# A small silu behind the first FFN's gelus, and a layernorm divided around the second join's copies

## The reference

```python
x = x + 0.5 * ffn(layernorm(x))            # first FFN  ("f1")
x = x + attn(layernorm(x))                 # gated delta rule, 8 heads, then a gelu MLP ("M")
x = x + 0.5 * ffn(layernorm(x))            # second FFN ("f2")

def ffn(x):                                # 128 -> 512 -> 512 -> 512 -> 128
    h = silu(tlin(x, w1)) * tlin(x, w2)
    h = gelu(tlin(h, h1)); h = gelu(tlin(h, h2))
    return tlin(h, w3)
```

## Time and profile before

| | us |
|---|---|
| median of 3 runs | 1373.7 (1373.3 to 1374.37) |
| the profiled execution, its own time | 1375.78 |
| its span, first to last instruction | 1374.0 |
| PE busy | 1343.2 |
| DVE busy | 836.8 |
| ACT busy | 664.2 |
| POOL busy | 569.3 |

### The profile page before, as it was taken

The page is one execution under the profiler, slowest core; times in us unless marked ns, Lnnn a source line. Parts: engine busy times, 40 slices in busy tenths (PEclk is TensorE's granted clock), DMA queues, the critical chain, the costliest instruction groups (busy, mean ns, idle before and its releaser), DMA issues.

```text
span 1374.0 us, 26425 instructions
## 1 busy us (share of the span) xinstructions
PE 1343.2 (98%) x10358; PEld 916.4 (67%) x10358; DVE 836.8 (61%) x2502; ACT 664.2 (48%) x1132; POOL 569.3 (41%) x646
## 2 busy tenths in 40 slices
PE   9999999999999999999999999999999999999998
PEld 5466686547855588556775568655686647865887
DVE  4477786456774577744776457755586446874441
ACT  2476656236642466425573256622566136652233
POOL 0038353822448144561346614385142832467100
PEclk9999999999999999999999999999999999999999
DMA  6030355332563234650447314463155532651000
GB/s 188 25 99 4 102 121 122 84 88 71 131 120 96 51 93 127 119 112 27 122 104 142 84 31 112 105 138 89 40 124 118 91 89 71 146 116 44 23 1 8
DMA packets 351980, 122.99 MB, mean 90 GB/s; under 512 B 317936, under 2 KB 333040, under 8 KB 351856
## 3 DMA queue, kind: packets, MB, share of 16 engines
q1 hardware_dynamic: 351856, 121.30, 37.5%
HBM read 78.53 MB, written 42.73 MB: 88 GB/s over the span
## 4 chain that ended last, share of the span: by engine, by line
PE 61%; issue 15%; POOL 13%; DVE 7%; DMA 3%; ACT 2%; SPq 0%; POOLq 0%; DVEq 0%; ACTq 0%
PE bank L1488 16%; PE bank L1615 8%; POOL blkT L632 5%; POOL blkP L629 5%; PE bank L1734 4%; PE bank L1725 4%; PE bank L1698 4%; PE bank L1640 3%; PE bank L1526 3%; PE bank L1715 3%; PE bank L1689 2%; PE bank L1706 2%; PE bank L1496 2%; POOL QET L613 2%; PE bank L1839 1%
## 5 line engine op out<-in xcount | busy, mean ns | idle before, releaser
L1488 PE MATMUL bank<-big,h 128*128 128x512 f32 (+1 forms) x1056 | 442.1, 569 | 2.7 <-DVE TB L1047 2.5
L1488 PEld LDWEIGHTS bank<-big,h 128*128 128x128 f32 x1056 | 196.0, 190 | 204.0 <-issue 194.1
L586 POOL TENSOR_TENSOR rnorm<-ssq,mhalf 128x16 f32<-128x16 f32 (+1 forms) x35 | 84.0, 2401 | 418.6 <-DVE ssq L893 418.6
L1615 PE MATMUL bank<-wqkv,nT 128*128 128x512 f32 x336 | 162.2, 603 | 1.1 <-ACT V L1309 1.1
L632 POOL TENSOR_TENSOR blkT<-blkT,blkP 128x31 f32<-128x31 f32 (+15 forms) x248 | 135.3, 546 | 19.4
L629 POOL TENSOR_TENSOR blkP<-blkA,blkT 128x31 f32<-128x31 f32 (+15 forms) x248 | 128.3, 517 | 28.8 <-DMA blkA<-blocks_out 10.0
L1526 PE MATMUL bank<-xT,w 128*128 128x512 f32 (+1 forms) x272 | 118.4, 577 | 11.6 <-DVE big L769 8.7
L1216 ACT ACTIVATE big<-bank,cols 128x512 f32<-128x512 f32 (+1 forms) x68 | 43.9, 662 | 133.5 <-PE bank L1488 95.4
L613 POOL TENSOR_TENSOR QET<-QET,sgf 128x1024 f32<-128x1024 f32 x24 | 56.5, 2353 | 99.7 <-DMA sgf<-e_rows 95.0
L1526 PEld LDWEIGHTS bank<-xT,w 128*128 128x128 f32 x272 | 48.7, 190 | 69.5 <-issue 41.5
L1224 ACT ACTIVATE big<-bank,cols 128x512 f32<-128x512 f32 (+1 forms) x68 | 44.1, 662 | 105.0 <-PE bank L1488 104.9
(11 more groups left out here) (244 smaller groups left out, 2543.0 us busy)
## 6 DMA issues: line engine op xcount, KB each, us to landing
rows_or_g<-g_rows SPq DMA_DIRECT2D x28, 512.0 KB, 4.9
q_rows<-mid SPq DMA_DIRECT2D x28, 512.0 KB, 5.0
QET<-q_rows SPq DMA_DIRECT2D x112, 128.0 KB, 4.2
k_rows<-R SPq DMA_DIRECT2D x27, 512.0 KB, 2.7
KT<-k_rows SPq DMA_DIRECT2D x108, 128.0 KB, 3.9
sgf<-e_rows SPq DMA_DIRECT2D x24, 512.0 KB, 4.6
blocks_out<-R SPq DMA_DIRECT2D x128, 32.0 KB, 1.7
blkA<-blocks_out SPq DMA_DIRECT2D x8, 512.0 KB, 3.8
```

The source lines that it names most:

```text
L586: pool.tensor_tensor(rnorm[:, heads_of], ssq[:, heads_of], mhalf[:, :].to_broadcast([128, heads_of.stop - heads_of.start]), ALU.pow).then_ ...
L1488: last = pe.matmul(bank[bk + i][:, t], w[:, k, 128 * o:128 * o + 128], src[:, k, t], start=(k == 0), stop=(k == KB - 1))
L1615: pe.matmul(bank[proj_bank(b, n)][:, :], nT[:, 128 * c:128 * c + 128], wqkv[:, i // 2, 512 * (i % 2):512 * (i % 2) + 512], start=True, sto ...
```

## The change

In ACT's stream a small silu is placed behind the last gelu of each first FFN of the loop (six places), and one more ahead of `input_T("f2", 6)` behind the loop. The one at the start of the program is the same call now. Each reads `ones` and writes the one column `warm`.

In DVE's stream `LN_F1` is divided. Its moments stay between `joined(t, 0)` and `joined(t, 1)`; the inverse and the rows come between `joined(t, 1)` and `joined(t, 2)` (five rounds, t = 1 to 5). Elsewhere `LN_F1` runs undivided.

```diff
             def LN_F1(b):
+                LN_F1_moments(b), LN_F1_rows(b)
+
+            def LN_F1_moments(b):
                 dve.wait_ge(ld_x, b * 48 + 48)
-                layernorm(ln_f["f1"], b, xin, xin)
+                moments(ln_f["f1"], b, xin)
+
+            def LN_F1_rows(b):
+                inverse(ln_f["f1"], b), normed(ln_f["f1"], b, xin, xin)
...
-                joined(t, 0), LN_F1(t + 2), joined(t, 1), joined(t, 2)
+                joined(t, 0), LN_F1_moments(t + 2), joined(t, 1), LN_F1_rows(t + 2), joined(t, 2)
...
+            def silu_table():
+
+                act.activation(warm[:, :], ones[:, :], ACT.Silu).then_inc(act_warm, 1)
+
             def F1(b):
 
                 act.wait_ge(m_down, b - 1)
-                gelus2("f1", b, 0), gelus2("f1", b, 1), gelus3("f1", b, 0), input_T("f2", b - 2), gelus3("f1", b, 1)
+                gelus2("f1", b, 0), gelus2("f1", b, 1), gelus3("f1", b, 0), input_T("f2", b - 2), gelus3("f1", b, 1), silu_table()
                 act.wait_ge(q_out, 16 * NC * (b - 1))
                 silus_F("f2", b - 2)
...
-            input_T("f2", B - 2)
+            silu_table(), input_T("f2", B - 2)
             act.wait_ge(q_out, 16 * NC * (B - 1))
```

More of the change, by code:

```diff
@@ L1460, in _ @@
             act.wait_ge(c_pool, 1)
-            act.activation(warm[:, :], ones[:, :], ACT.Silu).then_inc(act_warm, 1)
+            silu_table()
             act.wait_ge(ld_w, 3 * 16)
```

## The result

The change makes the kernel faster: the ratio to the kernel before is 0.9941, with a 95% interval of 0.993 to 0.9952. The medians are 1367.26 us and 1375.2 us. One of the seven runs of the kernel before took 2203.38 us; the ratio is formed without it. The ratio stands for 8.1 us; 8.0 us were forecast. The forecast time was 1365.7 us.

A forecast was written before the change was run, and what follows sets the result against it. PE was taken as the bound, busy 1343.2 of 1374.0 us, so only its idle gaps could shrink. Moved loads 4.2, seventh place 0 and divided layernorm 3.78 us took 1373.7 to 1365.7 us; range 1364.0 to 1369.9.

The forecast's parts named there:

- The moved load: ACT's silu table load moves into ACT's idle time before the second FFN's gates: 0.70 us in six rounds, 4.2 us.
- The seventh place: Small silu behind the loop: gain 0, upper bound 0.7 us; PE's wait at slot 11 about 0.9 us.
- The layernorm: Dividing LN_F1 on DVE removes PE's wait ahead of slot 12 in five rounds: 3.78 us, lower bound 2.49 us.
- No new wait: The joins' blocks are issued 10.7 us before join 0, so PE coming 0.7 us earlier meets no new wait.
- rival 2: PE's wait at slot 12 stays, DVE's moments meeting POOL's scaling for longer; 4.2 us gained, 1369.5 us; chance 4%.
- The sum: Whole kernel: 4.2 + 0 + 3.78 = 7.98 us off the 1373.7 us median, giving 1365.7 us.

## Why the prediction was right, and where not

- **The moved load.** Right in place and size. The load is hidden (7.92 us idle behind it), the small silu is 0.20 us between the bounds of 0 and 0.69, and PE gains 0.67 us a round where 0.70 us were summed. That a switch is worth only what PE waits for it was shown by taking the switches out.
- **The seventh place.** Right: no gain is shown. The waits stand at two slots and not at one, 0.55 us together and not 0.9 us.
- **The layernorm.** 3.80 us against 3.78 us. The moments end before join 1 in all rounds, and the rows end 0.67 us ahead of joined 2. The moments' end was put 7.06 us after join 0, with 0.86 us left; it came after 6.56 to 6.68 us in four rounds, with 1.24 to 1.36 us left, and after 4.54 us in round 4. The forecast added PE's 0.70 us in full, but the stop only grew to 2.2 or 2.3 us. This error was on the safe side.
- **No new wait.** Right: slot 6 does not wait for the blocks. The wait for the keys' load ahead of round 4's first FFN was 0.63 to 2.09 us in all kernels, 1.50 us before. All waits for that load come to 2.38 us before, and to 1.97 and 3.21 us in the two profiles of the changed kernel.
- **The price of rival 2.** Wrong. It priced the silus, with slot 12's wait kept, at 4.2 us and 1369.5 us. The term that was mis-sized is the kept wait: it grows, since POOL's scaling stands still while PE and the layernorm come sooner. The silus alone won 2.05 us by the timelines and 1.2 us by the measured times. The forecast itself did not rest on it. With the layernorm divided the stop still falls on the moments in four of five rounds, but there they have time to spare.
- **The sum.** 8.0 us forecast, 7.85 us by the places, 8.1 us by the ratio. That the 7.85 and the 8.1 us agree so closely is in part luck: the ratio's interval is 6.6 to 9.6 us, and the two profiled executions differ by 10.1 us.

Left open: what sets the wait for the keys' load. It stands ahead of round 4's first FFN and in the last round of every kernel, between 0.6 and 2.1 us, and elsewhere it is below 0.6 us or absent. It was not tried.

## What to carry to other kernels

Look for each idle time of the bound engine at one place and compare with the one round or batch where that place has none; the difference of start times gives the price more exactly than the idle time does. A wait that ends with another engine's stall can grow when the bound engine comes sooner, so part of a gain ahead of it may be lost until that wait goes too: two small edits can be worth more together than apart (7.85 us against 5.85 us here). Order the copies that the bound engine waits for ahead of any work that is not due.

## What the runs showed of the hardware

- One POOL TENSOR_TENSOR of 128x1024 stops a DVE instruction of four columns until it ends: 1.99 us in place of 0.17, and 2.23 us on a TENSOR_SCALAR, which has one input in SBUF. I had expected it of the form with two inputs; the second form was stopped as fully. BATCH_NORM_STATS2, also with one input in SBUF, was not stopped: ten of them took 6.02 to 6.03 us in each of five rounds, wherever the scaling of 2.35 us fell among them.
- Executions of one kernel differ by a few us, and much of it is the granted clock in short stretches. The repeated changed kernel was profiled at 1372.9 us of span against 1363.9 us. From 150 to 170 us it had:

```profile
150.00:170.00 20.00, 18.38 (x207) 14.19 (x208) 10.74 (x25) 10.88 (x18) 6.33 (x3) 0.74 0.29 88
```

The first profile of the same kernel had 1.00 there. From 154 to 162 us the granted clock was 0.50, the lower of the two levels (1.2 GHz), and a join of 64 records at 155.09 took 1.98 us in place of 1.16. PE came 3.7 us later to the first FFN of round 1 (225.11 against 221.39 us). Another 3.3 us went in the last joins of batch 7: from 1266 to 1268 us the clock was 0.50 again, and join 0 to join 2 took 15.29 us against 11.95. PE also paused there for 1.46 us without a wait that the profile shows. Between 150 and 160 us PE runs the last joins of batch 0, which are many small products with idle times between them (1.62, 0.95 and 1.12 us in the first profile). A single profile of this kernel therefore can't resolve 0.2%; differences of start times within a round can.
